# GpSimd issues the stores and loads of the pieces it splits, in the head attentions of a four-layer kernel

## The chip, the cores and the metric

The kernel is one program on one NeuronCore of a Trainium2 chip. The engines are named as in the profile: PE is TensorE, with its weight loads apart as PEld; DVE is VectorE; ACT is ScalarE; POOL is GpSimd; SP is SyncE, which computes nothing and only issues DMAs. An engine with a small q behind its name (SPq) stands for its instruction queue. The metric is the time of one execution in microseconds (us) on the device. Smaller is better.

## The reference, cut to what matters

Four layers act on x of 4 batches x 512 rows x 256. Each is a gated cross-attention to a context of 4 x 1601 rows, followed by a gated feed-forward part:

```
x = x + tanh(g_xattn[l]) * attention_l(layernorm(x), ctx)
x = x + tanh(g_ffn[l])   * ffn_l(layernorm(x))
```

The attentions of layers 0, 1 and 2 have 16 heads of width 16, and they are what the change is about:

```
q = (x @ Wq + bq) heads;  k = (ctx @ Wk + bk) heads;  v = (ctx @ Wv + bv) heads
layer 1:  q, k = rotary(q), rotary(k)
attention = softmax(q k^T * scale) v @ Wo + bo
```

Layer 3 has one wide head. The feed-forward parts are a quantised linear layer and three mixtures of experts. None of these is changed.

## The kernel before, in words

**Work.** A head attention goes through 4 batches b, and in a batch through 4 groups g of 4 heads. For a group, PE computes all scores once for the row maxima (matmuls `m`, L1289), DVE reduces them (`mxp`, L1172), and three rows with the negated maximum are sent by SP into the augmented queries (`qaug<-tm`, L1047, in layer 0 L894). Then PE computes the scores again, 128 keys at a time and transposed, with the maximum already subtracted (`s`, L1311, a unit called `s2`). ACT takes the exponential (`e_t`, L1403) and PE multiplies by the values (`pv`, L1325). There are 13 x 4 such `s2` units in a group. The maxima of a later group run between the `s2` units of the present one.

**Splitting.** Matmuls take bf16, so each f32 value of q and k is split into three bf16 pieces. `head_split` takes a tile of 128 x 512 from `kf` (and `kr`, for rotary), makes the pieces `ks`, and `split3` writes them (L1054 to L1057). There are two sets of these buffers (f = 0 and 1) and they alternate. `store_parts` then writes the pieces to DRAM, six slots for each row, with three DMAs (3, 2 and 1 slots, hence 384, 256 and 128 KB), and a later `fetch` reads them back into `kaug` and `qaug` in the order that the matmuls want. The tile of a batch b + 1 is split while batch b is computed. POOL splits nearly all: in layer 0 eight tiles of keys and two of queries for each further batch, in layers 1 and 2 two tiles of queries for each batch, and eight tiles of keys for batches 2 and 3. The keys of batches 0 and 1 of layers 1 and 2 are split ahead, during the layer before. In layer 0 the tile comes from PE and ACT. In layers 1 and 2 a tile of keys comes from DRAM (`kf<-keys`, in layer 1 also two halves of `kr<-keys`).

**Order.** `Plan` writes one list of units, and every engine goes through this list in order and does its part of each unit. SP's parts are all DMAs that are not ACT's: `turn` (`qaug<-tm`), `fetch`, the load of the next batch's values (at the unit `take` of the last group, `vn<-values`, L973), and `sum`, which moves the softmax denominators (`rc<-z`, L914) and the outputs (`ot<-z`, L917) once ACT has copied the group's result (`z`, L1415). After `sum` follow, at fixed places in the list: on DVE the reciprocal (`rec`, L1195), on ACT two DMAs (`low`: `sums<-rc`, `spread`: `ot<-sums`), and after each second group on DVE the normalisation (`norm`, L1199). DVE needs the landed DMA there, and the maxima stand behind it.

**SP and the splits.** At a `q` or `k` unit SP waits until POOL or DVE has split the tile, and issues the three stores. In layer 0 it does so at the tile's own unit. In layers 1 and 2 (`head_ready_sp`) it stores the tile of the unit before (`held`), and loads the tile of keys for the next unit (`load`). All of SP's later units wait behind. In layer 2 ACT also issues writes of zeros, 2 MB each, from a unit `take` of a batch after the first on (`xregion<-zero`), which go through ACT's queue q10 like `sums<-rc` and `ot<-sums`.

SP's queue is q1, POOL's is q0.

Of the kernel before, what the change touches and what calls it, by code (L numbers as in the profile page):

```python
# [12 lines left out]
B, T, D, S2 = 4, 512, 256, 1601  # L13
# [780 lines left out]
def head_dma_counts(a, name):  # L794

    a.dmas[name] = a.dmas.get(name, 0) + 1
    return a.dmas[name]


def head_stored(a, u):  # L800

    before = a.dmas.get(f"stored{u.f}", 0)
    a.dmas[f"stored{u.f}"] = before + len(RUNS)
    a.stored_of[u.kind, u.b, u.k, u.j] = (u.f, before, before + len(RUNS))


def head_sp(kn, a):
# [7 lines left out]
    split = {n: sig("split_" + n) for n in ("pool", "dve")}  # L815
    row = lambda t: t.rearrange("(c p) n -> p c n", p=P)
    n_of = lambda name: head_dma_counts(a, name)
    a.ctx_of, a.arrived, a.stored_of = {}, {}, {}
    ctx_until = [None] * 4
    if a.ready:  # L820
        head_ready_sp(kn, a, n_of)
# [25 lines left out]
    for at, u in enumerate(plan.units):  # L847
        if u.kind == "begin":
            if u.b:
                for n_c in range(2):  # L850
                    context(u.b, n_c, (n_c + 1) % 2)
            for by, n in set(a.arrived.values()):
                sp.wait_ge(sig(by, DMA).sem, sig(by, DMA).at(n))
        elif u.kind == "chunk":
            if u.b and u.k + 2 < len(CHUNKS):
                context(u.b, u.k + 2, (u.k + 3) % 2)
        elif u.kind in ("q", "k"):
            c0, n = CHUNKS[u.k] if u.kind == "k" else (0, T)
            dst = w["kparts"] if u.kind == "k" else w["qparts"]
            sp.wait_ge(split[u.by].sem, split[u.by].at(u.n + 1))  # L860
            store_parts(sp, u.kind, dst[P * u.j:P * u.j + P, :, c0:c0 + n], a.split_at[u.f][2][:, :, 0:n], stored[u.f].sem)
            head_stored(a, u)
        elif u.kind == "loads":
            mask_sp(kn, a)
            for t, src in ((a.wv, row(w["wv"])), (a.wo, row(w["wo"])), (a.bv, w["bv"]),
                           (a.bob, w["bo"].rearrange("(a n) -> a n", a=1).to_broadcast([P, D]))):
                sp.dma_start(t[:], src).then_inc(ld.sem, DMA)
        elif u.kind == "fetch":
            by = sig(u.by, DMA)
            for f in range(4):  # L870
                if a.dmas.get(f"stored{f}"):
                    sp.wait_ge(stored[f].sem, stored[f].at(a.dmas[f"stored{f}"]))
            if u.b:
                read = plan.find("s2", b=u.b - 1, g=u.g, k=KT - 1, j=HG - 1).s
                sp.wait_ge(s_full.sem, s_full.at(read + 1))
            h0, h1 = HG * HD * u.g, HG * HD * (u.g + u.k)
            for it, to, src in (("q", a.qaug, "qparts"), ("k", a.kaug, "kparts")):
                if it in u.what:
                    sp.dma_start(to[0:R_MASK, u.g:u.g + u.k, :, :].rearrange("p g j k -> p (g j) k"),
                                 w[src][h0:h1, :, :].rearrange("(h d) s k -> (d s) h k", d=HD)).then_inc(by.sem, DMA)  # L880
                    n_of(u.by)
            if a.mask is not None and "k" in u.what:
                for j in range(HG * u.k):
                    sp.dma_start(a.kaug[R_MASK:R_MASK + 1, u.g + j // HG, j % HG, :],
                                 a.mask[0][u.b:u.b + 1, :]).then_inc(by.sem, DMA)
                    n_of(u.by)
            for n in range(u.k):
                a.arrived[u.b, u.g + n, "k" if "k" in u.what else "q"] = (u.by, a.dmas[u.by])
        elif u.kind == "sum":
            head_sum_sp(kn, a, u)  # L890
        elif u.kind == "turn":
            sp.wait_ge(m_free.sem, m_free.at(u.m + 1))
            for k in range(3):
                sp.dma_start(a.qaug[R_MAX + k:R_MAX + k + 1, u.g, :, :].rearrange("a j (c q) -> a (j c) q", q=P),  # L894
                             a.tm[16 * k:16 * k + 16, :]).then_inc(td.sem, DMA)
# [24 lines left out]
def head_ready_sp(kn, a, n_of):  # L920
# [9 lines left out]
    row = lambda t: t.rearrange("(c p) n -> p c n", p=P)  # L930

    piece = lambda t: t.rearrange("(c t h i) s k -> c t h i s k", c=DC, t=2, h=H // DC)
    splits = [x for x in plan.units if x.kind in ("q", "k")]
    held = []

    def store():

        if held:
            x = held.pop()
            (c0, n), to = (CHUNKS[x.k], keys) if x.kind == "k" else ((0, T), queries)  # L940
            sp.wait_ge(split[x.by].sem, split[x.by].at(x.n + 1))
            store_parts(sp, x.kind, to[x.b, P * x.j:P * x.j + P, :, c0:c0 + n], a.split_at[x.f][2][:, :, 0:n], stored[x.f].sem)
            head_stored(a, x)

    def load(x):

        arrived, (c0, n) = sig(f"kl{x.f}", DMA), CHUNKS[x.k]
        kf, kr, _ = a.split_at[x.f]
        if rope and "tables_k" not in a.dmas:
            left_values()  # L950
            sp.dma_start(a.turn_k[:], a.rope[1]).then_inc(tables_k.sem, DMA)
            n_of("tables_k")
        src = kn.dram["keys"][x.b, P * x.j:P * x.j + P, c0:c0 + n]
        if x.b in LEFT:
            for f in range(a.p.RING):
                kept = sig(f"p_k{f}", DMA)
                sp.wait_ge(kept.sem, kept.at(a.p.stores[f]))
        sp.dma_start(kf[:, 0:n], src).then_inc(arrived.sem, DMA)
        for r in (0, P // 2) if rope else ():
            sp.dma_start(kr[r:r + P // 2, 0:n], src[P // 2 - r:P - r, :]).then_inc(arrived.sem, DMA)  # L960
        for _ in range(a.key_loads):
            n_of(f"kl{x.f}")

    def left_values():

# [13 lines left out]
    for u in plan.units:  # L979
# [19 lines left out]
            sp.wait_ge(filled.sem, filled.at(2))  # L999
            values_of(0)  # L1000
        elif u.kind in ("q", "k"):
            store()
            held.append(u)
            after = splits[splits.index(u) + 1:][0:1]
            for x in after:
                if x.kind == "k":
                    load(x)
        elif u.kind == "fetch":
            by = sig(u.by, DMA)
            if "q" in u.what:  # L1010
                store()
                for f in range(2):
                    last = max(n for (_, b, *_), (at, _, n) in a.stored_of.items() if b == u.b and at == f)
                    sp.wait_ge(stored[f].sem, stored[f].at(last))
            if u.b:
                read = plan.find("s2", b=u.b - 1, g=u.g, k=KT - 1, j=HG - 1).s
                sp.wait_ge(s_full.sem, s_full.at(read + 1))
# [42 lines left out]
def head_split(kn, a, u, eng, name):  # L1060

    own = name + "_own"
    s_free, done = kn.sema("s_free"), kn.sema("split_" + name)
    stored = kn.sema(f"stored{u.f}", DMA)
    n = CHUNKS[u.k][1] if u.kind == "k" else T
    kf, kr, ks = a.split_at[u.f]
    src, o = kf[:, 0:n], kr[:, 0:n]
# [14 lines left out]
        kn.settle(eng, own, eng.tensor_tensor(src, src, o, ALU.add))  # L1082
    if live:
        kn.settle(eng, own, eng.tensor_tensor(src, src, a.mask[1][:, u.b:u.b + 1].to_broadcast([P, n]), ALU.mult))
    before = a.stored_of[u.kind, u.b, u.k, u.j][1]
    if before:
        eng.wait_ge(stored.sem, stored.at(before))
    split3(kn, eng, own, kn.cst["ones"][:, 0:1].to_broadcast([P, n]), o, src, [ks[:, k, 0:n] for k in range(3)],
           a.rope is None and not live and not (a.ready and u.kind == "k")).then_inc(done.sem, 1)

# [1 line left out]
def head_pool(kn, a):  # L1092
    pool, plan = kn.nc.gpsimd, a.plan
    filled, b_made, biased = kn.sema("filled"), kn.sema("b_made"), kn.sema("biased")
    i = pool.memset(a.fill[0:R_ALL - R_MASK, 0:S2], 1.0)
    if not a.ready:
        i = pool.memset(a.fill[0:1, S2:2 * S2], 0.0)
# [11 lines left out]
    for u in plan.units:  # L1109
        if u.kind == "stats":  # L1110
            norm_pool(kn, "n", *FIRST_TILES[u.k], u.k)
        elif u.kind in ("q", "k") and u.by == "pool":
            head_split(kn, a, u, pool, "pool")
        elif u.kind == "bias":

            pool.wait_ge(b_made.sem, b_made.at(3))
            for b in range(B):
                xb = kn.x[:, TT * b:TT * b + TT, :]
                pool.tensor_tensor(xb, xb, a.bob[:].rearrange("p (t n) -> p t n", t=1).to_broadcast([P, TT, D]),
                                   ALU.add).then_inc(biased.sem, 1)  # L1120
# [216 lines left out]
def head_act(kn, a):  # L1337
# [10 lines left out]
    for u in plan.units:  # L1348
# [8 lines left out]
        elif u.kind == "q" or u.kind == "k" and not a.ready:  # L1357
# [8 lines left out]
            for t, (to, b_) in enumerate(zip((kf, kr), bias)):  # L1366
                slot = a.s_slot[(u.s + t) % 3]
                act.wait_ge(s_full.sem, s_full.at(u.s + t + 1))
                i = act.activation(to[:, 0:n], slot[:, 0:n], ACT.Identity, bias=b_[:, u.j:u.j + 1], scale=mul)
                if direct:  # L1370
                    before = a.stored_of[u.kind, u.b, u.k, u.j][1]
                    if before:
                        stored = kn.sema(f"stored{u.f}", DMA)
                        act.wait_ge(stored.sem, stored.at(before))
                    i = act.activation(ks[:, 0, 0:n], slot[:, 0:n], ACT.Identity, bias=b_[:, u.j:u.j + 1], scale=mul)  # L1375
                i.then_inc(s_free.sem, 1)
        elif u.kind == "prep":
# [1724 lines left out]
```

## Time and profile before

| | us |
|---|---|
| median of 3 runs | 3853.88 |
| the runs | 3853.88, 3861.94, 3851.54 |
| span of the profiled execution | 3829.6 |
| median less the span | 24.3 |
| PE busy, share of the span | 3401.9, 89% |
| DVE busy | 2159.4, 56% |
| ACT busy | 2034.7, 53% |
| POOL busy | 745.3, 19% |

The span runs from the first to the last instruction in the profile. What lies around it (start and end of the execution) isn't in the trace; the profiled execution gives no other time of its own, so the difference to the median of the runs stands for it. The attention of layer 0 lies between about 100 and 860 us, that of layer 1 between 1030 and 1805 us, and that of layer 2 between 2110 and 2880 us.

### The profile page before, as it was taken

Reading aid. Unit: us, or ns where it says so; the run is one execution under the profiler, and the core shown is the slowest. Engines: PE = TensorE matmul, PEld = TensorE weight load, DVE = VectorE, ACT = ScalarE, POOL = GpSimd, SP = SyncE. Lnnn points to the kernel's source line nnn. Section 1 sums busy time; section 2 is a strip of 40 time slices with the busy share of each in tenths; the row PEclk is TensorE's granted clock in tenths of the full one; section 3 lists DMA queues with packets and bytes.
Section 4 is the critical chain, followed back from the end, with each engine's and each line's share of the span. In section 5 each row is a group of like instructions: output and inputs, shape, how many; then the busy total and the mean of one; then the engine's idle time right before and its main releaser. Section 6 shows DMA issues by size and latency. Waiting matters only on the chain.

```text
span 3829.6 us, 52360 instructions
## 1 busy us (share of the span) xinstructions
PE 3401.9 (89%) x18396; PEld 1770.7 (46%) x18396; DVE 2159.4 (56%) x3463; ACT 2034.7 (53%) x4490; POOL 745.3 (19%) x768
## 2 busy tenths in 40 slices
PE   5899999988689989997899799989987979987997
PEld 3333333325432323332697322323326956687996
DVE  6767676736757777873402477767743033264333
ACT  2566666763236666775333266667772322244664
POOL 2211111003635331000302141210002010022332
PEclk8999999999779999998899799999998989999998
DMA  8132424105664443211874655644208521042554
GB/s 194 42 103 61 106 57 110 26 14 187 178 182 124 101 111 82 45 24 46 267 231 154 185 152 118 171 112 103 77 10 285 186 78 69 1 143 92 184 186 167
DMA packets 314686, 456.02 MB, mean 119 GB/s; under 512 B 66315, under 2 KB 234195, under 8 KB 312251
## 3 DMA queue, kind: packets, MB, share of 16 engines
q1 hardware_dynamic: 233206, 285.70, 27.5%
q0 software_dynamic: 29568, 104.65, 8.2%
q10 hardware_dynamic: 51653, 62.32, 5.8%
q8 instruction: 150, 2.46, 0.3%
q14 instruction: 109, 0.89, 0.1%
HBM read 292.46 MB, written 153.91 MB: 117 GB/s over the span
## 4 chain that ended last, share of the span: by engine, by line
PE 67%; DVE 13%; DMA 8%; ACT 4%; POOL 3%; issue 3%; SPq 1%; ACTq 0%; another core or an unknown queue 0%; POOLq 0%; DVEq 0%
PE pv L1325 14%; PE m L1289 11%; PE s L1311 9%; DVE mxp L1172 9%; PE h L2811 5%; PE y L2819 5%; PE h L2385 4%; PE y L2394 4%; PE y L1791 2%; PE s L1771 2%; PE s L1256 2%; DMA sums<-rc 2%; ACT e_t L1403 1%; DMA ot<-sums 1%; PE m L1333 1%
## 5 line engine op out<-in xcount | busy, mean ns | idle before, releaser
L1172 DVE TENSOR_REDUCE mxp<-m 128x1 f32<-128x802 f32 x1536 | 1447.8, 987 | 526.9 <-PE m L1289 523.2
L1403 ACT ACTIVATE e_t<-s 128x512 f32<-128x512 f32 (+1 forms) x2496 | 1340.3, 599 | 552.0 <-PE s L1311 532.9
L1289 PE MATMUL m<-kaug,qaug 97*128 97x401 bf16 x3072 | 811.6, 347 | 97.5 <-DVE mxp L1172 51.6
L1311 PE MATMUL s<-qaug,kaug 100*128 100x512 bf16 (+1 forms) x2496 | 859.4, 386 | 34.1 <-ACT e_t L1403 29.0
L1325 PE MATMUL pv<-e_t,v 128*32 128x512 f32 (+1 forms) x4992 | 670.3, 609 | 0.2
L1311 PEld LDWEIGHTS s<-qaug,kaug 100*128 100x128 bf16 (+1 forms) x2496 | 229.4, 99 | 733.8 <-ACT e_t L1403 519.6
L1289 PEld LDWEIGHTS m<-kaug,qaug 97*128 97x128 bf16 x3072 | 273.4, 99 | 506.7 <-DVE mxp L1172 265.2
L127 POOL TENSOR_TENSOR rstd<-rstd,mhalf 128x16 f32<-128x16 f32 (+2 forms) x9 | 24.2, 2690 | 1150.8 <-DVE rstd L120 1150.8
L2881 ACT ACTIVATE ez<-h,b 128x128 f32<-128x128 f32 x440 | 120.1, 388 | 159.7 <-PE h L2811 159.7
L1325 PEld LDWEIGHTS pv<-e_t,v 128*32 128x32 f32 (+1 forms) x4992 | 98.6, 108 | 214.9 <-ACT e_t L1403 161.3
L2272 DVE SCALAR_TENSOR_TENSOR y<-y,b 128x256 f32<-128x256 f32 x39 | 16.6, 425 | 303.0 <-PE y L2394 303.0
L2683 DVE TENSOR_SCALAR ez<-ez 128x1024 f32<-128x1024 f32 x55 | 38.2, 694 | 224.6 <-ACT z L2881 224.6
L1055 POOL TENSOR_TENSOR kr<-kf,ks 128x512 f32<-128x512 f32 (+1 forms) x78 | 78.4, 1005 | 432.2 <-ACT ks L1375 428.1
L2468 ACT ACTIVATE hT<-h,b 128x128 f32<-128x128 f32 x312 | 84.9, 383 | 128.1 <-PE h L2385 128.0
L2385 PE MATMUL h<-xtT,w 128*128 128x128 f32 x1248 | 149.3, 279 | 0.3 <-ACT xtT L2485 0.3
L2819 PE MATMUL y<-w,hT 128*128 x624 | 143.0, 383 | 5.8 <-DVE hT L2684 5.8
L2811 PE MATMUL h<-xtT,w 128*128 128x128 f32 x1248 | 147.3, 277 | 0.0
L2385 PEld LDWEIGHTS h<-xtT,w 128*128 128x128 f32 x1248 | 146.3, 196 | 0.6 <-ACT xtT L2485 0.5
L2811 PEld LDWEIGHTS h<-xtT,w 128*128 128x128 f32 x1248 | 144.1, 194 | 0.1
L2394 PE MATMUL y<-w,hT 128*128 x624 | 140.9, 379 | 0.0
L2819 PEld LDWEIGHTS y<-w,hT 128*128 128x128 f32 x624 | 116.8, 192 | 20.9 <-issue 6.4
L2881 ACT ACTIVATE z<-h,b 128x128 f32<-128x128 f32 x440 | 122.8, 453 | 0.0
(377 smaller groups left out, 3616.2 us busy)
## 6 DMA issues: line engine op xcount, KB each, us to landing
w<-in_L_w POOLq DMA_DIRECT2D x78, 1024.0 KB, 5.4
w<-in_L_w SPq DMA_DIRECT2D x24, 1024.0 KB, 12.7
xregion<-zero ACTq DMA_DIRECT2D x10, 2056.0 KB, 12.2
kaug<-kparts SPq DMA_DIRECT2D x16, 1200.8 KB
kaug<-kready SPq DMA_DIRECT2D x32, 600.4 KB
kaug<-kready SPq DMA_DIRECT2D x16, 1200.8 KB
vn<-values SPq DMA_DIRECT2D x8, 1536.0 KB
values<-p_vb ACTq DMA_DIRECT2D x21, 512.0 KB
```

Of the source, the lines that this page charges most:

```text
L1055: kn.settle(eng, own, eng.tensor_tensor(rest, src, parts[0], ALU.subtract))
L1172: dve.tensor_reduce(a.mxp[:, u.g % 2, half, n:n + 1], a.m_slot[u.m % 2][:].rearrange("p (a n) -> p a n", a=2)[:, :, 0:PIECE + 1], AX.XY, A ...
L1289: m = pe.matmul(slot[:, 512 * k:512 * k + PIECE + 1], a.qaug[0:R_MAX, u.g, j, P * qc:P * qc + P], a.kaug[0:R_MAX, u.g, j, k0:k0 + PIECE + ...
L1311: pe.matmul(slot[0:KW[u.k], :], a.kaug[0:R_ALL, u.g, u.j, P * u.k:P * u.k + KW[u.k]], a.qaug[0:R_ALL, u.g, u.j, :], start=True, stop=True) ...
L1325: m = pe.matmul(a.pv[32 * j:32 * j + 32, :], a.v[0:KW[u.k], u.k, u.g, VW * j:VW * j + 32], a.e_t[0:KW[u.k], u.n % 2, j, :], start=u.k == 0 ...
L1403: act.activation(a.e_t[0:KW[u.k], e % 2, u.j, :], a.s_slot[u.s % 3][0:KW[u.k], :], ACT.Exp).then_inc(s_free.sem, 1)
L2385: m = pe.matmul(a.h_slot[i % 2][:, P * f:P * f + P], a.w1[:, w1_at, c, P * f:P * f + P], xT(c), start=c == 0, stop=c == DC - 1)
L2394: m = pe.matmul(a.y_slot[i % 2][:, 0:D], a.hT[:, i % 2, f, :], w2(f), start=f == 0, stop=f == FC - 1)
L2468: t = act.activation(a.hT[:, p, f, :], slot[:, P * f:P * f + P], func, bias=bias(f))
L2811: m = pe.matmul(a.h_slot[i % 2][:, P * f:P * f + P], w1[:, c, P * f:P * f + P], xT(c), start=c == 0, stop=c == DC - 1)
L2819: m = pe.matmul(a.y_slot[i % 2][:, 0:D], a.hT[:, i % 2, f, :], w2(f), start=f == 0, stop=f == FC - 1)
L2881: t = act.activation(to[:, p, P * f:P * f + P], slot[:, P * f:P * f + P], func, bias=bias(f))
```

## The change

SP no longer stores the tiles that POOL splits, and no longer loads keys. POOL does both itself, right behind the split. `head_stores_itself` is true for every tile that POOL splits, other than those of batch 0 in layer 0. After a split and its stores, in layers 1 and 2, POOL issues the load of the tile after the next, which goes into the buffers that it has just read. SP's `fetch` waits for the new semaphores `pooled0` and `pooled1` beside the old ones. In layers 1 and 2 SP now stores the one tile that DVE splits at its own unit. Loads and stores are the same in number, size and place; three stores a tile, one load (three in layer 1) a tile of keys, and once the rotary table `turn_k`, go from q1 to q0.

```diff
+def head_stores_itself(a, u):
+    return u.by == "pool" and (a.ready or u.b > 0)
+
+def head_store_pool(kn, a, u):
+    pool, done, stored = kn.nc.gpsimd, kn.sema("split_pool"), kn.sema(f"pooled{u.f}", DMA)
...
+    pool.wait_ge(done.sem, done.at(u.n + 1))
+    store_parts(pool, u.kind, dst, a.split_at[u.f][2][:, :, 0:n], stored.sem)
+
+def head_load_pool(kn, a, x):
...
+    if rope and "tables_k" not in a.dmas:
...
+        pool.dma_start(a.turn_k[:], a.rope[1]).then_inc(kn.sema("tables_k", DMA).sem, DMA)
...
+    pool.dma_start(kf[:, 0:n], src).then_inc(arrived.sem, DMA)
+    for r in (0, P // 2) if rope else ():
+        pool.dma_start(kr[r:r + P // 2, 0:n], src[P // 2 - r:P - r, :]).then_inc(arrived.sem, DMA)
...
 head_sp, layer 0:
-            sp.wait_ge(split[u.by].sem, split[u.by].at(u.n + 1))
-            store_parts(sp, u.kind, dst[...], a.split_at[u.f][2][:, :, 0:n], stored[u.f].sem)
+            if not head_stores_itself(a, u):
+                sp.wait_ge(...); store_parts(sp, ...)
             head_stored(a, u)
...
         elif u.kind == "fetch":
-                if a.dmas.get(f"stored{f}"):
+                for name in (f"stored{f}", f"pooled{f}"):
...
 head_ready_sp, layers 1 and 2:
         elif u.kind in ("q", "k"):
-            store()
-            held.append(u)
-            after = splits[splits.index(u) + 1:][0:1]
-            for x in after:
-                if x.kind == "k":
-                    load(x)
+            store(u)
...
 head_pool:
             head_split(kn, a, u, pool, "pool")
+            if head_stores_itself(a, u):
+                head_store_pool(kn, a, u)
+            for x in splits[splits.index(u) + 2:][0:1] if a.ready else ():
+                if x.kind == "k":
+                    head_load_pool(kn, a, x)
```

## Rows read from the trace of the kernel before

**Rows 1.** The page's first line

```profile
span 3829.6 us, 52360 instructions
```

**Rows 2.** SP's own waits, all of the run: engine line, releaser, us in total, times, longest us

```profile
SPq L94 <- POOL ks L1057: 258.2, 44, 19.5
```

**Rows 3.** Timeline of SP: start us, us, line, operation; the issues of `rc<-z`

```profile
1297.75 0.60 SPq L914 DMA_DIRECT2D rc<-z  x1
...
1354.34 0.59 SPq L914 DMA_DIRECT2D rc<-z  x1
...
1397.29 0.59 SPq L914 DMA_DIRECT2D rc<-z  x1
...
1475.26 0.60 SPq L914 DMA_DIRECT2D rc<-z  x1
...
1566.31 0.61 SPq L914 DMA_DIRECT2D rc<-z  x1
```

**Rows 4.** Timeline of ACT at 1347 us, the copy of `z`

```profile
1347.00 0.59 ACT L1415 COPY z<-pv 128x512 f32<-128x512 f32 x1 [0.76 <-PE pv L1325]
```

**Rows 5.** Timeline of SP, 1340 to 1363 us

```profile
1349.65 2.31 SPq L94 DMA_DIRECT2D kready<-ks  x3
```

**Rows 6.** Timeline of DVE, three of the reciprocals; in brackets idle time before

```profile
176.60 0.25 DVE L1195 RECIPROCAL rc<-rc 128x16 f32<-128x16 f32 x1 [1.38 <-DMA rc<-z]
...
1186.97 0.25 DVE L1195 RECIPROCAL rc<-rc 128x16 f32<-128x16 f32 x1 [2.18 <-DMA rc<-z]
...
1364.06 0.25 DVE L1195 RECIPROCAL rc<-rc 128x16 f32<-128x16 f32 x1 [7.71 <-DMA rc<-z]
```

**Rows 7.** Timeline of POOL, 221 to 240 us

```profile
224.32 0.31 POOL L1057 TENSOR_TENSOR ks<-kr,ks 128x65 bf16<-128x65 f32 x1
...
229.88 1.16 POOL L1055 TENSOR_TENSOR kr<-kf,ks 128x512 f32<-128x512 f32 x1 [5.25 <-ACT ks L1375]
...
235.84 1.16 POOL L1057 TENSOR_TENSOR ks<-kr,ks 128x512 bf16<-128x512 f32 x1
```

**Rows 8.** Timeline of SP, 222 to 243 us

```profile
233.42 5.48 SPq L94 DMA_DIRECT2D qparts<-ks  x6
...
241.19 0.47 SPq L879 DMA_DIRECT2D kaug<-kparts  x1
```

**Rows 9.** Waits of PE up to 3000 us: us in total, times, longest us

```profile
PE m L1289 <- DMA kaug<-kparts: 22.4, 4, 11.4
```

**Rows 10.** Groups of POOL by line: busy us, mean ns, idle before

```profile
L2618 POOL DMA_DIRECT2D w<-in_L_w x39 | 28.2, 722 | 13.5 <-PE h L2811 11.7 <-issue 1.5
...
L2626 POOL DMA_DIRECT2D xt<-xregion x39 | 22.1, 566 | 26.9 <-issue 26.9
```

**Rows 11.** Timeline of POOL, 3504 to 3513 us

```profile
3507.81 0.55 POOL L2626 DMA_DIRECT2D xt<-xregion  x1 [0.42 <-issue]
```

**Rows 12.** DMA issues of the whole run: count, KB each, median us to landing

```profile
yback<-y,dest POOLq DMA_INDIRECT x39, 2.4
...
qparts<-ks SPq DMA_DIRECT2D x8, 128.0 KB, 2.7
```

**Rows 13.** Timeline of SP, the two loads of the next batch's values, layer 1

```profile
1329.29 0.58 SPq L973 DMA_DIRECT2D vn<-values  x1
...
1493.81 0.60 SPq L973 DMA_DIRECT2D vn<-values  x1
```

**Rows 14.** Waits, 1494:1510, 2380:2402 and 2555:2580 us

```profile
DVE ot L1199 <- DMA ot<-sums: 2.5, 1, 2.5
...
DVE ot L1199 <- DMA ot<-sums: 7.6, 1, 7.6
...
DVE ot L1199 <- DMA ot<-sums: 10.6, 1, 10.6
```

**Rows 15.** DMA queues from 2383 to 2392 us: packets, MB, share of 16 engines

```profile
q10 hardware_dynamic: 1649, 1.70, 90.5%
...
q1 hardware_dynamic: 319, 0.44, 20.0%
```

More of the change, by code:

```diff
@@ L800, in head_stored @@
 def head_stored(a, u):
-    before = a.dmas.get(f"stored{u.f}", 0)
-    a.dmas[f"stored{u.f}"] = before + len(RUNS)
-    a.stored_of[u.kind, u.b, u.k, u.j] = (u.f, before, before + len(RUNS))
+    name = f"pooled{u.f}" if head_stores_itself(a, u) else f"stored{u.f}"
+    n = a.dmas.get(name, 0) + len(RUNS)
+    a.dmas[name] = n
+    a.stored_of[u.kind, u.b, u.k, u.j] = (name, n, a.stored_last.get(u.f))
+    a.stored_last[u.f] = (name, n)
+def head_stores_itself(a, u):
+    return u.by == "pool" and (a.ready or u.b > 0)
+def head_store_pool(kn, a, u):
+    pool, done, stored = kn.nc.gpsimd, kn.sema("split_pool"), kn.sema(f"pooled{u.f}", DMA)
+    (c0, n), to = (CHUNKS[u.k], "k") if u.kind == "k" else ((0, T), "q")
+    if a.ready:
+        dst = kn.dram["kready" if to == "k" else "qready"][u.b, P * u.j:P * u.j + P, :, c0:c0 + n]
+    else:
+        dst = a.w[to + "parts"][P * u.j:P * u.j + P, :, c0:c0 + n]
+    pool.wait_ge(done.sem, done.at(u.n + 1))
+    store_parts(pool, u.kind, dst, a.split_at[u.f][2][:, :, 0:n], stored.sem)
+def head_load_pool(kn, a, x):
+    pool, arrived, (c0, n), rope = kn.nc.gpsimd, kn.sema(f"kl{x.f}", DMA), CHUNKS[x.k], a.rope is not None
+    kf, kr, _ = a.split_at[x.f]
+    if rope and "tables_k" not in a.dmas:
+        for f in range(2):
+            kept = kn.sema(f"p_v{f}", DMA)
+            pool.wait_ge(kept.sem, kept.at(len(a.p.chunks) // 2))
+        pool.dma_start(a.turn_k[:], a.rope[1]).then_inc(kn.sema("tables_k", DMA).sem, DMA)
+        head_dma_counts(a, "tables_k")
+    src = kn.dram["keys"][x.b, P * x.j:P * x.j + P, c0:c0 + n]
+    if x.b in LEFT:
+        for f in range(a.p.RING):
+            kept = kn.sema(f"p_k{f}", DMA)
+            pool.wait_ge(kept.sem, kept.at(a.p.stores[f]))
+    pool.dma_start(kf[:, 0:n], src).then_inc(arrived.sem, DMA)
+    for r in (0, P // 2) if rope else ():
+        pool.dma_start(kr[r:r + P // 2, 0:n], src[P // 2 - r:P - r, :]).then_inc(arrived.sem, DMA)
+    for _ in range(a.key_loads):
+        head_dma_counts(a, f"kl{x.f}")
 def head_sp(kn, a):
@@ L859, in head_sp @@
             dst = w["kparts"] if u.kind == "k" else w["qparts"]
-            sp.wait_ge(split[u.by].sem, split[u.by].at(u.n + 1))
-            store_parts(sp, u.kind, dst[P * u.j:P * u.j + P, :, c0:c0 + n], a.split_at[u.f][2][:, :, 0:n], stored[u.f].sem)
+            if not head_stores_itself(a, u):
+                sp.wait_ge(split[u.by].sem, split[u.by].at(u.n + 1))
+                store_parts(sp, u.kind, dst[P * u.j:P * u.j + P, :, c0:c0 + n], a.split_at[u.f][2][:, :, 0:n], stored[u.f].sem)
             head_stored(a, u)
@@ L870, in head_sp @@
             for f in range(4):
-                if a.dmas.get(f"stored{f}"):
-                    sp.wait_ge(stored[f].sem, stored[f].at(a.dmas[f"stored{f}"]))
+                for name in (f"stored{f}", f"pooled{f}"):
+                    if a.dmas.get(name):
+                        sp.wait_ge(sig(name, DMA).sem, sig(name, DMA).at(a.dmas[name]))
             if u.b:
@@ L932, in head_ready_sp, with store @@
     piece = lambda t: t.rearrange("(c t h i) s k -> c t h i s k", c=DC, t=2, h=H // DC)
[L933 to L939, printed above, removed]
+    def store(x):
+        if not head_stores_itself(a, x):
             (c0, n), to = (CHUNKS[x.k], keys) if x.kind == "k" else ((0, T), queries)
@@ L942, in store @@
             store_parts(sp, x.kind, to[x.b, P * x.j:P * x.j + P, :, c0:c0 + n], a.split_at[x.f][2][:, :, 0:n], stored[x.f].sem)
[L943 to L962, printed above, removed]
+        head_stored(a, x)
     def left_values():
@@ L1010, in head_ready_sp @@
             if "q" in u.what:
-                store()
                 for f in range(2):
-                    last = max(n for (_, b, *_), (at, _, n) in a.stored_of.items() if b == u.b and at == f)
-                    sp.wait_ge(stored[f].sem, stored[f].at(last))
+                    for name in (f"stored{f}", f"pooled{f}"):
+                        of_b = [n for (_, b, *_), (at, n, _) in a.stored_of.items() if b == u.b and at == name]
+                        if of_b:
+                            sp.wait_ge(sig(name, DMA).sem, sig(name, DMA).at(max(of_b)))
             if u.b:
@@ L1063, in head_split @@
     s_free, done = kn.sema("s_free"), kn.sema("split_" + name)
-    stored = kn.sema(f"stored{u.f}", DMA)
     n = CHUNKS[u.k][1] if u.kind == "k" else T
@@ L1084, in head_split @@
         kn.settle(eng, own, eng.tensor_tensor(src, src, a.mask[1][:, u.b:u.b + 1].to_broadcast([P, n]), ALU.mult))
-    before = a.stored_of[u.kind, u.b, u.k, u.j][1]
+    before = a.stored_of[u.kind, u.b, u.k, u.j][2]
     if before:
-        eng.wait_ge(stored.sem, stored.at(before))
+        stored = kn.sema(before[0], DMA)
+        eng.wait_ge(stored.sem, stored.at(before[1]))
     split3(kn, eng, own, kn.cst["ones"][:, 0:1].to_broadcast([P, n]), o, src, [ks[:, k, 0:n] for k in range(3)],
@@ L1094, in head_pool @@
     filled, b_made, biased = kn.sema("filled"), kn.sema("b_made"), kn.sema("biased")
+    splits = [x for x in plan.units if x.kind in ("q", "k")]
     i = pool.memset(a.fill[0:R_ALL - R_MASK, 0:S2], 1.0)
@@ L1370, in head_act @@
                 if direct:
-                    before = a.stored_of[u.kind, u.b, u.k, u.j][1]
+                    before = a.stored_of[u.kind, u.b, u.k, u.j][2]
                     if before:
-                        stored = kn.sema(f"stored{u.f}", DMA)
-                        act.wait_ge(stored.sem, stored.at(before))
+                        stored = kn.sema(before[0], DMA)
+                        act.wait_ge(stored.sem, stored.at(before[1]))
                     i = act.activation(ks[:, 0, 0:n], slot[:, 0:n], ACT.Identity, bias=b_[:, u.j:u.j + 1], scale=mul)
```

2 lines of the change are left out of this document (1 added, 1 removed).

## The prediction

> **What bounds the kernel now.** The page comes first: the span is 3829.6 us [rows 1], PE is busy for 89% of it and POOL for 19%, so more work on POOL is not in itself a cost. Then the waits by engine. SP's own list shows that it stood 258.2 us in 44 waits for a split of POOL [rows 2]. That is not a cost yet: SP is a queue, and what counts is which of its later DMAs somebody needed. So I went through the issues of `rc<-z` in the timeline of SP. ACT had `z` ready at 1347.59 [rows 4], and SP issued the move only at 1354.34 [rows 3], because at 1349.65 it was still storing pieces that POOL had just finished [rows 5], with a fetch behind them. DVE then stood 7.71 us before its reciprocal [rows 6], the maxima behind it stood too, and PE and ACT ran dry. Two smaller waits of the kind are at 1187 us (2.18 us) and 176.6 us (1.38 us) [rows 6]. The other 40-odd sums aren't late by SP.
>
> The second thing to see is a chain in layer 0 that has no slack. POOL splits the two query tiles of the next batch directly after each other: the first from 229.88, the second ends at 235.84 + 1.16 = 237.00 [rows 7]. SP issues six stores in 5.48 us from 233.42 on, thus to 238.90, and 2.3 us later, at 241.19, it can issue the fetch [rows 8]. PE waits for this fetch: the list of PE's waits has 22.4 us in four for `kaug<-kparts`, of which the longest, 11.4 us, is the start of the kernel. The other three, 11.0 us together or 3.7 each, are the fetches for batches 1 to 3 [rows 9]. Whatever delays that fetch is added to the end.
>
> **Cost 1, the chain of layer 0.** POOL must now issue three DMAs between the first query tile and the second. The trace of before has no such store from POOL. The nearest rows are its loads: 566 ns for 128 rows (`xt`) and 722 ns for 256 rows (`w`) [rows 10]. By these I put the three stores, with 384, 256 and 128 runs of 1 KB, at 0.88 + 0.72 + 0.57 = 2.2 us. Between two DMAs POOL shows 0.42 us idle [rows 11], so three cost 3.4 us. From below, three at 0.57 without a gap are 1.7 us. From above, three like the largest with gaps are 3.9 us. I take 3.4, as the gap is in the row.
> This hits at three points. (a) Before the queries come two short tiles of keys; the second ended at 224.32 + 0.31 = 224.63 [rows 7]. With two stores of 3.4 us before the queries POOL is free at 231.4 and not before 229.88, so 1.5 us late (0 to 2.6). (b) The second query tile starts 3.4 us later (1.7 to 3.9). (c) Its own stores take POOL until 3.4 us after the split, where SP was done after 238.90 - 237.00 = 1.9 us: 1.5 us more (0 to 2.0). I take the landing as unchanged: POOL's indirect DMA of 128 KB lands 2.4 us after its start, SP's store of 128 KB after 2.7 [rows 12]. Sum 6.4 us for a batch (1.7 to 8.5), three batches: **+19.2 us** (5 to 25.5). Nothing covers it, since PE waits already.
>
> The Trainium skill, "DMA: Bandwidth & Descriptors", sections "Issuing engine by pattern" and "Specifications", sends simple loads and stores to SyncE and gives about 1 us to the first byte from GpSimd and 0.6 from SyncE; by that the landing would be 0.4 us later, an estimate of 1.2 us more for three batches. Rows 12 show no such difference, and I don't count it.
>
> **Gain 1, sums in layer 0.** SP no longer stands before `sum` of group 0. The wait of 1.38 us [rows 6] goes, in three batches: **-4.2 us** (0 to -5).
>
> **Gain 2 and its give-back, layer 1.** Without the wait SP issues the fetch as soon as the previous group's scores are done, and `rc<-z` at 1347.6. It had 8.7 us to land (DVE was ready at 1364.06 - 7.71 = 1356.35). The wait of 7.71 goes. But SP also reaches the load of the next batch's values earlier. In batch 0 to 1 it stood behind the splits until 1329.29, in batch 1 to 2, where no keys are split between, it went out at 1493.81 [rows 13], next to the DMA for the normalisation, and DVE stood 2.5 us for that [rows 14]. After the change both boundaries look alike, so the second is the measure of the first. From the sum of the last group to the second sum after it: 1397.29 - 1297.75 = 99.5 us in the first, 1566.31 - 1475.26 = 91.1 in the second [rows 3]. The difference holds the gain and what is given back: **-8.5 us** (8.5 + 2.5 = -11 if the values don't collide, -2 if the sum is late anyway). By the same account a DVE wait of 7.71 us cost 11, 1.4 times itself, so for the 2.18 us at 1187 [rows 6] I take 1.4 x 2.18: **-3 us** (0 to -4).
>
> **Cost 2, layer 2.** No sum is late here. But the values go out earlier in batch 0 to 1 as well. DVE waits 7.6 us there for the normalisation's DMA and 10.6 at the next boundary, where the values already go out beside it [rows 14]. The difference is 3.0; half of it I take as real, since PE and ACT have a little work queued: **+1.5 us** (0 to 3).
>
> **Cost 3, POOL's transfers among the others.** SP paced the loads of keys; now POOL runs eight tiles back to back, and stores its query tiles at once. At the two boundaries of layer 2 this falls into the clearing writes. **+2 us** (0 to 9, which is 1 MB or so more in front of each of two landings and of ACT's waits for `sums<-rc`).
>
> Free edits: POOL's other DMAs (some 260 outside the layer 0 chain) cost some 1.1 us each, and lie in POOL's idle four fifths of the span; where that cover is gone it shows as in cost 1. The first tile's store at the start of layers 1 and 2 is some 1.5 us later under the preparing matmuls. SP's two more waits in `fetch` cost nothing by themselves.
>
> **Sum.** 19.2 - 4.2 - 8.5 - 3 + 1.5 + 2 = +7.0 us on 3829.6 gives 3836.6 in the span. The median of the runs shown is 24.3 us above the span of this execution, and I add the same: **3861 us**.
>
> **Rivals.**
> *The stores of POOL are nearly free (faster).* One mechanism, at the second query tile of layer 0: if descriptors are made while POOL computes, cost 1 falls to its lower bound of 5 us, and the gains remain: 5 - 4.2 - 8.5 - 3 = -10.7, and with the full 11 for gain 2, -13.2: 3841 us. It decides as soon as a query tile starts less than 2 us after the last one's end. For it: POOL's DMA rows last only 0.6 to 0.7 us. Against it: the gap of 0.42 between them. 0.18.
> *Transfers in turn (slower).* Until now SP's ring was held up behind ACT's: while q10 had 90.5% of the DMA engines from 2383 to 2392 us, q1 had 20% [rows 15]. If POOL's ring takes a part beside both, the landings that DVE and ACT wait for in layers 1 and 2 go late, cost 3 is its upper 9: 3868, and up to 3876 if layer 1's sums are pushed out as well. It decides when `ot<-sums` lands over 2 us later than now. 0.20. The Trainium skill, "DMA: Bandwidth & Descriptors", section "Queues, rings and completion order", says that each DMA engine goes round the queues with work, a packet of each. By that rule POOL's transfers slow SP's and ACT's evenly. The trace agrees only in part, as rows 15 are far from even.
> *It doesn't do what it says in layer 1.* The fetch stands before `rc<-z` in the same queue still, and with POOL's stores beside it the sum lands after 1356.35. Gain 2 shrinks to 2 and the small one to 0: +7 + 6.5 + 3 = 3870 us. Against it: the sums from 1397 us on wait for nothing with the same fetch ahead. 0.12.
>
> **Numbers.** My forecast has 0.50, with its own range 3852 to 3870. About 0.3% (11.6 us) is what a measurement of this kernel tells from no change: 3842 to 3865. The forecast lies inside with 0.37 and above with 0.13; the free stores are faster with 0.15 and the same with 0.03; the transfers in turn slower with 0.18 and the same with 0.02; the late sum slower with 0.09 and the same with 0.03. Faster 0.15, same 0.45, slower 0.40. The range of 8 in 10 reaches from 3845, inside the first rival, to 3877.
>
> **What would show it.** Cost 1: a gap of some 3.4 us on POOL between the two query tiles at 230 to 240 us, the fetch at about 247 and not 241, and the three waits of PE for `kaug<-kparts` some 6 us longer each. Gain 2: no wait of DVE before the reciprocal at about 1360, 91 us and not 99.5 over these two groups. Cost 2: `vn<-values` at the first boundary right after ACT's copy, and a wait for `ot<-sums` of 2 us in layer 1 and about 10 in layer 2. It would be wrong if POOL's DMA costs far from 1.1 us, if the store lands much later than SP's, or if POOL's burst of key tiles makes other waits than those named.

## The result, and the profile after

The changed kernel takes 3888.45 us (median of 4 runs, 3883.22 to 3893.53) against 3855.32 (4 runs) for the kernel before: ratio 1.0077 with a 95% interval of 1.0057 to 1.0098, thus 22 to 38 us slower. The forecast was 3861 us, with 3845 to 3877 as its range. The sign of its sum (+7) was right. Its size was not, and the time lies above the range.

The page's first rows of the kernel after, the pages' rows of two queues (packets, MB, share of 16 engines; first before, then after) and SP's waits after:

```profile
span 3882.0 us, 52370 instructions
...
PE 3419.7 (88%) x18396; PEld 1777.1 (46%) x18396; DVE 2162.8 (56%) x3463; ACT 2033.7 (52%) x4490; POOL 941.3 (24%) x1061
```

```profile
q1 hardware_dynamic: 233206, 285.70, 27.5%
q0 software_dynamic: 29568, 104.65, 8.2%
```

```profile
q1 hardware_dynamic: 163878, 224.05, 21.9%
q0 software_dynamic: 49520, 166.30, 13.1%
```

```profile
SPq L94 <- POOL ks L1073: 17.5, 1, 17.5
```

The change does what it says. SP's waits for splits of POOL went from 44 to 1 [rows 2]. POOL has 196 us more of work (745.3 before), and about 62 MB moved from SP's queue (q1) to POOL's (q0). In q1 these bytes were 69328 packets, in q0 they are 19952: the same data goes in some 3.5 times fewer and larger packets. That matters below.

**Two spans that can't be subtracted.** The spans of the two traces differ by 52.4 us [rows 1], the medians by 33. The profiled run after took 3883.22 us with its span of 3882.0, so only 1.2 us lie outside a span. So the 24.3 us that the prediction added as "what lies around" didn't lie around it: with 1.2 us around its span of 3829.6 the profiled execution of before lies 21 us under the fastest timed run of before, 3851.54. It was a fast one, by luck or because it ran on another chip; the record doesn't say which. The control below shows where it was faster.

**Layer 0.** PE's waits for the fetch, and POOL's timeline at the same place as [rows 7]:

```profile
PE m L1311 <- DMA kaug<-kparts: 33.2, 4, 13.2
```

```profile
229.27 2.08 POOL L94 DMA_DIRECT2D kparts<-ks  x3 [0.29 <-POOL ks L1073]
232.15 1.15 POOL L1071 TENSOR_TENSOR kr<-kf,ks 128x512 f32<-128x512 f32 x1 [0.80 <-ACT ks L1397]
...
235.95 2.10 POOL L94 DMA_DIRECT2D qparts<-ks  x3 [0.30 <-POOL ks L1073]
238.06 1.17 POOL L1071 TENSOR_TENSOR kr<-kf,ks 128x512 f32<-128x512 f32 x1
...
240.42 1.15 POOL L1073 TENSOR_TENSOR ks<-kr,ks 128x512 bf16<-128x512 f32 x1
241.88 2.08 POOL L94 DMA_DIRECT2D qparts<-ks  x3 [0.30 <-POOL ks L1073]
```

and SP's issue of the fetch, which answers to [rows 8]:

```profile
246.76 0.47 SPq L922 DMA_DIRECT2D kaug<-kparts  x1
```

The waits grew from 22.4 us [rows 9] to 33.2. The longest of the four is the start of the kernel, which the change doesn't touch (11.4, then 13.2 us); the other three, the fetches of the chain, grew from 11.0 to 20.0 us. Three stores take POOL 2.1 us back to back, with one gap of 0.3 before the first and none between them. The stores of the key tiles cost nothing: at 232.15 POOL had already waited 0.80 us for ACT.

**Layer 1.** Issues of `rc<-z` and `vn<-values` in SP's timeline, then DVE's timeline:

```profile
1303.68 0.62 SPq L957 DMA_DIRECT2D rc<-z  x1
1321.13 0.34 SPq L993 DMA_DIRECT2D vn<-values  x1
...
1360.56 0.61 SPq L957 DMA_DIRECT2D rc<-z  x1
1401.33 0.62 SPq L957 DMA_DIRECT2D rc<-z  x1
```

```profile
1332.85 0.69 DVE L1221 TENSOR_TENSOR ot<-ot 128x512 f32<-128x512 f32 x1 [4.61 <-DMA ot<-sums]
1371.46 0.25 DVE L1217 RECIPROCAL rc<-rc 128x16 f32<-128x16 f32 x1 [2.15 <-DMA rc<-z]
```

`rc<-z` goes out as soon as `z` is there, and DVE's wait for it fell from 7.71 us [rows 6] to 2.15. But the values now go out at 1321, beside the normalisation's DMA, and DVE stands 4.61 us for that, where the kernel before shows no such wait. The two groups take 1401.33 - 1303.68 = 97.7 us. They took 99.5 [rows 3]. By ACT's copies of `z`, the group over the boundary grew from 49.9 to 56.9 us and the next one fell from 49.7 to 40.8: the gain came, and most of it was given back.

**Layer 2.** Most of the cost is here, as the experiments show. ACT's timeline over one group boundary, POOL's stores there, and the DMA queues in four windows of it (2270 to 2276, 2278 to 2286, and of the latter 2278 to 2279 and 2280 to 2281 us; the times of packets overlap, so shares can add up to over 100%):

```profile
2268.71 0.66 ACTq L1463 DMA_DIRECT2D xregion<-zero  x1
...
2272.20 0.33 ACTq L1445 DMA_DIRECT2D sums<-rc  x1
...
2288.07 0.57 ACTq L1452 DMA_DIRECT2D ot<-sums  x1
2288.69 2.56 ACT L1425 ACTIVATE e_t<-s 128x512 f32<-128x512 f32 x5 [9.78 <-DMA sums<-rc]
```

```profile
2269.48 2.09 POOL L94 DMA_DIRECT2D kready<-ks  x3 [0.30 <-POOL ks L1073]
...
2277.07 0.81 POOL L94 DMA_DIRECT2D kready<-ks  x1 [0.30 <-POOL ks L1073]
```

```profile
q10 hardware_dynamic: 1421, 1.46, 108.8%
```

```profile
q0 software_dynamic: 456, 1.39, 75.6%
q10 hardware_dynamic: 602, 0.47, 30.0%
```

```profile
q0 software_dynamic: 41, 0.16, 79.3%
q10 hardware_dynamic: 44, 0.05, 28.7%
```

```profile
q0 software_dynamic: 63, 0.19, 77.1%
q10 hardware_dynamic: 61, 0.06, 28.4%
```

ACT writes 2 MB of zeros (`xregion<-zero`) and, behind it in the same queue (q10), the 8 KB of sums. A few instructions on, `ot<-sums` waits until these have landed, and the exponentials stand behind it. From 2270 to 2276 us only ACT's queue moves, 1.46 MB, though POOL issued 768 KB of pieces at 2269.48. Then both move, and the counts of packets are even (41 to 44, 63 to 61), but POOL's packets are three to four times as large: ACT's queue, at 0.19 MB a us just before (2275 to 2276 us), is down to 0.05. `ot<-sums` goes out 15.9 us after the issue of the sums (2288.07 - 2272.20), and ACT stands 9.78 us.

What that does to PE is seen in PE's timeline and in the windows (us, PE busy and count, granted clock, DMA share, GB/s):

```profile
2289.34 1.10 PE L1333 MATMUL s<-qaug,kaug 100*128 100x512 bf16 x2 [8.47 <-ACT e_t L1425]
```

```profile
2268.00:2280.00 12.00, 11.81 (x71) 1.00 0.95 207
...
2288.00:2292.00 4.00, 2.66 (x12) 0.50 0.22 58
2292.00:2296.00 4.00, 3.74 (x24) 0.86 0.11 27
```

PE had a granted clock of 1.00 (2.4 GHz) while it was busy, stood 8.47 us, and came back at 0.50 (1.2 GHz). So this stall cost its own length and a slow stretch after it. The same happens at the first group boundary of the next batch (ACT stands 7.74 us before 2480.28); at the other boundaries between groups of this layer ACT stands 2.95 to 3.32 us for the sums.

### The profile page after: what moved, and what is told of

Read it like the earlier page. It is cut to its first block, busy times and chain, and to the rows that moved or that the text cites. A ratio compares the mean times of both kernels' runs of the same rounds, so it can differ in the third digit from the quotient of the medians.

```text
span 3882.0 us, 52370 instructions
## 1 busy us (share of the span) xinstructions
PE 3419.7 (88%) x18396; PEld 1777.1 (46%) x18396; DVE 2162.8 (56%) x3463; ACT 2033.7 (52%) x4490; POOL 941.3 (24%) x1061
## 3 DMA queue, kind: packets, MB, share of 16 engines
q0 software_dynamic: 49520, 166.30, 13.1%
## 4 chain that ended last, share of the span: by engine, by line
PE 67%; DVE 14%; DMA 9%; ACT 4%; issue 3%; POOL 2%; SPq 1%; ACTq 0%; POOLq 0%; DVEq 0%
PE pv L1347 14%; PE m L1311 11%; PE s L1333 9%; DVE mxp L1194 9%; PE h L2833 5%; PE y L2841 5%; PE h L2407 4%; PE y L2416 3%; PE y L1813 2%; PE s L1793 2%; DMA sums<-rc 2%; PE s L1278 2%; DMA ot<-sums 2%; ACT e_t L1425 1%; PE m L1355 1%
## 5 line engine op out<-in xcount | busy, mean ns | idle before, releaser
L127 POOL TENSOR_TENSOR rstd<-rstd,mhalf 128x16 f32<-128x16 f32 (+2 forms) x9 | 24.3, 2696 | 1150.2 <-DVE rstd L120 1150.2
## 6 DMA issues: line engine op xcount, KB each, us to landing
xregion<-zero ACTq DMA_DIRECT2D x10, 2056.0 KB, 12.7
```

## The experiments

All variants are written into the changed kernel with a switch for each layer; the ratios are to the kernel before, run on the same chip. Its median there was 3867 to 3872 us, and not 3855, so experiments are compared by these ratios. The kernel after itself wasn't run on these chips.

```diff
 def head_stores_itself(a, u):
-    return u.by == "pool" and (a.ready or u.b > 0)
+    return u.by == "pool" and (a.ready or u.b > 0) and u.kind in POOL_STORES[a.layer]
...
-            for x in splits[splits.index(u) + 2:][0:1] if a.ready else ():
+            for x in splits[splits.index(u) + 2:][0:1] if a.ready and POOL_LOADS[a.layer] else ():
```

Where a switch is off, SP has its old `store` and `load` back, in the old order.

**1. Control.** `POOL_STORES = {0: '', 1: '', 2: ''}`, `POOL_LOADS` off.

> All stores and loads back on SyncE in the three attentions, written into the kernel after the change with the same edits that the partial variants use. Both theories: within 0.3% of the kernel before (ratio 0.997 to 1.003). Its profile is a second execution of the old order of work: if its span is near 3850 and not near 3830, some 20 of the 52 us by which the two traces differ are a matter of the execution; if a control is over 0.3% from before, the other variants are to be read against it and not against before.

Measured: 3869.46 us, ratio 1.0003 (0.9994 to 1.0012). The switches cost nothing that shows. The span of its profile is 3863.3 us, with the same order of work as the 3829.6 of before. The first group boundary of layer 2 in both, first the kernel before, then the control (ACT's timeline):

```profile
2266.95 2.56 ACT L1403 ACTIVATE e_t<-s 128x512 f32<-128x512 f32 x5 [3.08 <-DMA sums<-rc]
```

```profile
2249.80 0.58 ACT L1485 COPY z<-pv 128x512 f32<-128x512 f32 x1 [0.76 <-PE pv L1395]
...
2274.02 2.56 ACT L1473 ACTIVATE e_t<-s 128x512 f32<-128x512 f32 x5 [3.96 <-DMA sums<-rc]
...
2292.77 0.58 ACT L1485 COPY z<-pv 128x512 f32<-128x512 f32 x1 [0.76 <-PE pv L1395]
```

ACT stood 0.9 us longer in the control. PE stood 1.78 us there in the kernel before and 2.66 in the control (PE's timeline), and the windows just after it read:

```profile
2268.00:2272.00 4.00, 3.66 (x22) 1.00 0.08 31
```

```profile
2274.00:2278.00 4.00, 3.23 (x15) 0.81 0.10 35
```

The first is the kernel before, which kept its clock; the second is the control, which did not. Its group took 43.0 us from one `z` to the next, and that of before 40.9. From its first to its last `z` the attention of layer 2 is 23 us longer in the control's trace (647 against 624), some two thirds of the 34 us between the spans. The length of the stall alone doesn't decide, though. In the nine traces with the clears early (before, after, experiments 1 to 6 and 9) ACT stands 70 times for `sums<-rc` in this layer, and PE behind it, each time from a clock of 1.00. After 16 of these stalls of PE (1.05 to 2.48 us) the clock stayed at 1.00, after the other 54 (1.65 us and more) it fell within the next 8 us: between 1.65 and 2.48 us both happened. The groups took 40.2 to 41.6 us where it stayed and 42.1 us or more where it fell. In the profile of before it stayed in all six, in the control it fell in all eight. The clears landed a little earlier in the former, too (12.2 us against 13.1 in the median). So the trace of before hid how little room was left in this layer.

**2. Layer 0 alone.** `POOL_STORES = {0: 'qk', 1: '', 2: ''}`

> Only the attention of layer 0 has GpSimd's own stores. Theory A (the cost lies in the transfers of layer 2): about +11 us, the growth of the offset in layer 0 by the trace, ratio 1.003. Theory B (the prediction: the cost is the chain of layer 0, three fetches each 6.4 us late, less 4.2): +15 us, ratio 1.004. Both: PE's three waits for kaug<-kparts together 8 to 20 us longer; layer 2 keeps the group times of before.

Measured: 3875.35 us, ratio 1.0021 (1.0012 to 1.0029), +8 us (4.6 to 11). PE's waits for the fetch, which were 23.2 us in the control:

```profile
PE m L1359 <- DMA kaug<-kparts: 34.0, 4, 14.0
```

Without the start of the kernel (13.8 us in the control, 14.0 here) three fetches grew from 9.4 to 20.0 us, 3.5 for each. The chain of layer 0 is real, and a little over half the size that was forecast.

**3. Layer 1 alone.** `{0: '', 1: 'qk', 2: ''}`, with the loads of layer 1

> Only the attention of layer 1 has GpSimd's stores and loads. Theory A: 0 to -4 us, since the trace shows -3.4 over this attention, ratio 0.999 to 1.000. Theory B: -11.5 us, ratio 0.997, as the late sum is gone and the give-back is small.

Measured: 3865.29 us, ratio 0.9994 (0.9982 to 1.0007), -2 us (-7 to +3). The attention of this layer is 6 us shorter in its trace than in the control's. A gain of 11.5 us is excluded.

**4. Layer 2 alone.** `{0: '', 1: '', 2: 'qk'}`, with the loads of layer 2

> Only the attention of layer 2 has GpSimd's stores and loads. Theory A (a third ring takes its turns at the DMA engines beside ScalarE's clearing writes of 2 MB, and the small moves queued behind these land late): +20 to +34 us, ratio 1.005 to 1.009, with ACT's waits for sums<-rc of 5 us and more in several groups. Theory B: +3 us, ratio 1.001, and the rest of the 34 us that the trace shows in this layer is a matter of the execution.

Measured: 3890.91 us, ratio 1.0061 (1.0048 to 1.0074), +24 us (19 to 29). Experiments 2 to 4 add up to 30 us (to 26 if each is counted from the control), of the 33 (22 to 38) of the whole change. In the trace the layer is 16 us longer from its first to its last `z` than in the control: the first groups of batches 0 and 1 by 6.8 and 7.7 us, the groups over the two batch boundaries, where the forecast saw the cost, by 2.2 and 3.2, and the others 4 us shorter together. The first boundary again (ACT's timeline; 49.8 us between the two `z`):

```profile
2260.67 0.59 ACT L1485 COPY z<-pv 128x512 f32<-128x512 f32 x1 [0.76 <-PE pv L1395]
...
2291.39 2.55 ACT L1473 ACTIVATE e_t<-s 128x512 f32<-128x512 f32 x5 [10.46 <-DMA sums<-rc]
...
2310.48 0.59 ACT L1485 COPY z<-pv 128x512 f32<-128x512 f32 x1 [0.76 <-PE pv L1395]
```

and POOL's store of the tile that falls behind the clear:

```profile
2271.54 2.12 POOL L94 DMA_DIRECT2D kready<-ks  x3 [0.30 <-POOL ks L1120]
```

**5 and 6. Layer 2, stores alone and loads alone.** `{2: 'qk'}` with the loads off, and `{2: ''}` with the loads on, each behind the split that frees its buffer.

> Layer 2 alone, and only the stores of the split pieces are GpSimd's; SyncE loads the keys, each after the previous split, as before. Theory A1 (the extra ring's bytes and runs beside ScalarE's clears cost; the stores are about four fifths of the DMAs and of the small runs): +15 to +20 us of the 24 that layer 2 alone cost. Theory A2 (the pace: GpSimd loads its next keys at once and so runs its eight tiles in a burst, where SyncE spaced them): 0 to +5 us.

> Layer 2 alone, and only the loads of the keys are GpSimd's; SyncE stores the pieces after its waits, as before. Theory A1: +3 to +8 us, the smaller part. Theory A2: +15 to +20 us, if the pace of the loads is what matters.

Measured: stores 3878.25 us, ratio 1.003 (1.0019 to 1.0041), +12; loads 3869.76, ratio 1.0004 (0.9993 to 1.0015), +2. The two don't add up to 24: some 10 us are missing, a little more than the scatter of the three together. Neither account was right alone: the stores are the larger part, but SP's loads pace them. With SP's loads, which stand in its queue behind other work, the first boundary takes 44.2 us in place of 49.8, and ACT stands 4.80 us for the sums and not 10.46. In experiment 4 POOL stores tiles 0.8 and 8.4 us after the issue of the clear, in experiment 5 5.6 and 12.7 us after it. So the burst, one tile straight after the other with stores and loads, seems to be what puts two whole tiles beside the clear; that is read from one boundary.

**7 and 8. The clears behind the small moves.** In ACT's queue the write of zeros goes behind `ot<-sums`, with the stores by POOL in layer 2 (7) and with everything by SP (8):

```diff
-            if a.clears and u.b:
-                clear_act(kn, a, (u.b - 1) * NG + u.g)
...
         elif u.kind == "spread":
             head_spread_act(kn, a, u)
+            if a.clears:
+                clear_act(kn, a, u.n)
```

> Layer 2 alone, stores and loads by GpSimd, but ScalarE issues its clearing write of a group after the move of the sums and not ahead of it, so that sums<-rc and ot<-sums have no 2 MB in front of them in their own queue. Theory A (the three rings meet, but what makes it dear is the clear ahead of the small moves): at most +5 us over the kernel with late clears alone, against +24 with early clears. Rival (the third ring slows everything alike): still +15 to +25 over the kernel with late clears alone.

> The old order of work (SyncE stores and loads everything) with ScalarE's clears late. It is the base for the run before it. Theory A: faster than before by 10 to 25 us, as DVE's waits of 7.6 and 10.6 us for ot<-sums in layer 2 go with what they drag along. Rival (those waits come from values and keys in SyncE's queue, not from the clears): within 3 us of before.

Measured: (8) 3823.22 us, ratio 0.988 (0.9865 to 0.9896), 46 us faster than before (40 to 52), more than either account expected. In the traces the layer is 47 us shorter than in the control from its first to its last `z` (599.9 against 647.2); half of it lies in the two groups over the batch boundaries (60.0 to 45.9 and 56.7 to 47.2 us), where `ot<-sums` was behind a clear. (7) 3840.84 us, ratio 0.9933 (0.992 to 0.9945): 17.6 us slower than (8). So the clear ahead of the sums is dear in itself, but taking it away doesn't take away the cost of POOL's transfers. That part of my account fell. PE's timeline at the first boundary of (7) and the windows behind it:

```profile
2295.34 0.61 PE L1381 MATMUL s<-qaug,kaug 100*128 100x512 bf16 x1 [3.45 <-DMA qaug<-tm]
```

```profile
2283.00:2291.00 8.00, 7.91 (x50) 2.74 (x50) 6.15 (x9) 5.69 (x11) 0.32 (x1) 1.00 1.00 122
2295.00:2299.00 4.00, 3.67 (x10) 1.34 (x10) 1.99 (x2) 2.02 (x4) 0.00 (x0) 0.50 1.04 220
2299.00:2303.00 4.00, 4.00 (x15) 0.97 (x15) 1.64 (x2) 1.59 (x4) 0.00 (x0) 0.50 0.43 102
```

Columns: us, busy of PE, PEld, DVE, ACT and POOL, granted clock, DMA share, GB/s. Now it is SP's move of the maxima, `qaug<-tm`, that lands late: 9.8 us after its issue in the median, with the clear and POOL's last pieces outstanding, and 6.1 us after it in (8). PE stands 3.45 us, and then its clock is 0.50 for two windows. In (8) the same wait is 0.16 us.

**9 and 10. POOL holds its stores at the sums.** Before it stores a tile, POOL waits until the last group's sums have landed, with the clears early (9) and late (10):

```diff
     pool.wait_ge(done.sem, done.at(u.n + 1))
+    if a.layer == 2:
+        sums = [x for x in a.plan.units[:a.plan.units.index(u)] if x.kind == "spread"]
+        if sums:
+            summed = kn.sema("summed", DMA)
+            pool.wait_ge(summed.sem, summed.at(3 * sums[-1].n + 2))
     store_parts(...)
```

> Layer 2 alone, stores and loads by GpSimd, but the store of a tile whose place in the order of the units is behind a group's sums waits until these sums have landed; so no piece is written between ScalarE's clear and sums<-rc in the groups where keys are split. Theory A (dear are the stores that fall between a clear and the landing of sums<-rc): of the +24 us of layer 2 alone at most +8 are left, and the group from the first to the second z of the layer takes about 43 us, as in the control, and not 49.8. Theory U (GpSimd's transfers cost what they cost wherever they fall): still +18 to +28, the lateness only appears at another landing.

> The same with ScalarE's clears behind the move of the sums. Both the third ring and the clear are then behind the small moves. The base is the kernel with late clears alone (about 44 us below before), against which GpSimd's unguarded transfers cost 18. Theory A: 0 to +8 us over that base, about 35 to 44 below before. Theory U: again +14 to +22 over the base, because the pieces now land late behind the clear and the fetch waits for them.

Measured: (9) 3877.69 us, ratio 1.0016 (1.0006 to 1.0026): +6 us (2 to 10) where the unguarded kernel had +24. POOL stood for the sums, and at this boundary ACT stood no longer than in the control (POOL's, then ACT's timeline):

```profile
2282.00 2.12 POOL L94 DMA_DIRECT2D kready<-ks  x3 [15.45 <-DMA sums<-rc]
```

```profile
2282.10 2.56 ACT L1478 ACTIVATE e_t<-s 128x512 f32<-128x512 f32 x5 [3.70 <-DMA sums<-rc]
```

The boundary took 43.3 us. The same bytes by the same queue, sent 13 us later (23.9 us after the `z`, and not 10.9), cost a quarter. So it was their place, between a clear and the landing of the sums, that made some 18 of the 24 us. (10) 3838.08 us, ratio 0.9919 (0.9906 to 0.9933): 15 us over (8), and 5 us under (7) with intervals that overlap. So with late clears the guard does little: at the first boundary PE again stands for `qaug<-tm`, 4.39 us. Theory U names the fetch there, and that isn't what the trace shows.

**11 and 12. The parts put together.** Clears late, layer 1 by POOL, layer 2 by SP; layer 0 with the key tiles by POOL (11, `{0: 'k', 1: 'qk', 2: ''}`) or all by SP (12).

> A version put together from the parts: layer 0 with the stores of the key tiles alone by GpSimd (the query tiles, which the fetch waits for, by SyncE), layer 1 by GpSimd, layer 2 by SyncE, ScalarE's clears late. If the parts add up: late clears -44, layer 1 -2 to -6, key tiles of layer 0 -2 to 0: 44 to 52 us below before, ratio 0.987 to 0.989. If GpSimd's transfers cost in layer 1 as they do in layer 2: above -44.

> Layer 1 by GpSimd, layers 0 and 2 by SyncE, clears late. Against the run before it this leaves out the key tiles of layer 0. By the account of the prediction (a wait of 1.4 us before the reciprocal, three times) it is 4 us slower than that run; by the account of the trace of layer 0 alone (2 us of gain in all) 2 us slower, too little to tell. Below before by 44 to 50 us.

Measured: (11) 3817.49 us, ratio 0.9867 (0.9852 to 0.9882), 51 us faster than before. (12) 3818.36 us, ratio 0.9865 (0.985 to 0.988). Both beat both kernels. They can't be told from each other, so no gain or loss from the key tiles of layer 0 shows. Against (8) they are 5 us better, with intervals that overlap. Nearly the whole gain is the place of the clears.

## Why the prediction was wrong

- **Cost 3, the step that failed.** "+2 us (0 to 9)" for POOL's transfers among the others. Layer 2 alone measured +24 (19 to 29), against the +3.5 of costs 2 and 3 together. The mechanism is the rival "Transfers in turn", which had 0.20 and at most 9 us; the measured time is above even its 3876. I priced it as a megabyte or so in front of two landings. Three things were missing: most of it falls on ACT's wait for `sums<-rc` at the first group boundary of two batches, where keys are split, and not at the two batch boundaries; what stands in line there is already 2 MB of zeros, with ACT waiting 3 us; and a stall of PE of 8 to 9 us is followed by a stretch at half clock.
- **Rows 15 were read as protection.** ACT's queue had 90.5% beside SP's 20.0% there, and I took it that ACT's queue holds its own. The trace after shows both in the same clear: POOL's queue moves nothing for 6 us with 768 KB issued, and then has 75.6% against 30.0. The rule of the Trainium skill, "DMA: Bandwidth & Descriptors", section "Queues, rings and completion order", that an engine takes a packet of each queue in turn, was nearer to the effect than my reading of one window. From 2278 to 2281 us the trace bears it out, with 41 packets to 44, 58 to 59 and 63 to 61; even in packets is not even in bytes, and there the two queues differ by more than three to one. From 2270 to 2276 us, with 1421 packets to none, it doesn't. The trace of before has the same: SP issued a store at 2383.84, and its queue had no packets from 2385 to 2390 us.
- **Cost 1, layer 0: right chain, half the size.** Forecast +19.2 us, measured 9.0 in PE's three waits (10.6 in layer 0 alone over the control). (a) the key tiles' stores: 1.5 forecast, 0 shown, as POOL waited for ACT after them. (b) between the query tiles: 3.4 forecast. From the start of the first query tile to the end of the second it is 241.57 - 232.15 = 9.42 us and was 7.12 [rows 7], thus 2.3. (c) from there to the issue of the fetch 5.19 us and before 4.19 [rows 7, 8]: 1.0, forecast 1.5. The gap of 0.42 us of rows 11 was the wrong row: three stores have one gap of 0.3. The landing, taken as unchanged, is hardly later: for 384, 256 and 128 KB of `qparts` 3.1, 3.2 and 2.8 us in the median from POOL (kernel after) against 2.6, 2.9 and 2.7 from SP (control).
- **Gain 1.** Forecast -4.2 us. Layer 0 alone costs 8.2 where the waits cost 10.6, so about -2.4. That the waits of 1.38 us went is shown, but their price can't be separated from the scatter.
- **Gain 2, layer 1.** Forecast -11.5 us, measured -2 (-7 to +3). SP's wait before `rc<-z` went, as forecast. The give-back was read off the second boundary, with a wait of DVE of 2.5 us; the wait is 4.61 at the first one, whose group grew by 7.0 us, and 3.5 at the second, whose group grew by 1.8 (trace after). And 2.15 us of DVE's wait for `rc<-z` stayed, which was the third rival in part. The small gain of 3 us came: the group at 1187 us went from 43.7 to 39.7.
- **Cost 2.** +1.5 us. DVE's waits for `ot<-sums` in layer 2 are 6.2 and 13.0 us, in sum 19.2 against 18.2 [rows 14]. That looks right, but the control, with SP's old order, has 10.0 and 10.8, in sum 20.8: no such cost shows. One by one they are not as forecast either ("about 10" for each).
- **The 24.3 us.** They weren't around the span but inside it. The sum itself, 7 against 33, is 26 us short: 20 of it in layer 2, 10 in layer 1, less 7 in layer 0. That leaves 3, which the runs don't resolve. As the 24.3 only carried the sum from a fast execution to the median, they did no harm to it.

What stays open: why POOL's queue moves nothing for the first 6 us of a clear and then a packet for each of ACT's, and what the remaining 6 us of the guarded kernel are. Its two batch boundaries are 2 to 3 us longer than the control's. Nor is it separated how much of the cost lies in the moment of the stores and how much in POOL's queue, with its larger packets: in the control SP issues no store between a clear and the landing of the sums at the first boundary, and no run lets SP send the same burst there.

## What to carry to other kernels

A queue that stands behind somebody's wait is also a pacer: before taking the wait away, look at what its transfers will run beside, and which landing an in-order engine waits for there. The bytes didn't change here, only when, by which queue and in what packets they went, and a guard that held them behind that landing took back three quarters of the cost. And where a bulk write with no deadline stands ahead of an 8 KB move that an engine waits for, put it behind: that was worth 46 us, more than the change cost.

## What the runs showed of the hardware that was not expected

- Two queues share the DMA engines in no fixed proportion: with stores of POOL's queue outstanding, ACT's queue had 1421 packets to none in 6 us, and a few us later 44 to 41. The same bytes were 69328 packets in SP's queue and 19952 in POOL's, so at even counts POOL's queue moved 0.16 MB to ACT's 0.05.
- A stall of PE from full clock of 1.78 us left it at 1.00, one of 2.66 was followed by a window at 0.81, one of 3.45 and one of 8.47 by windows at 0.50. So 0.9 us more of waiting went with 2 us more for a group, in two executions of the same order of work. Over 70 such stalls, those between 1.65 and 2.48 us went either way.
- A store that POOL issues takes it 0.70 us in the mean (384, 256 and 128 KB: 0.81, 0.73, 0.57), and three mostly go back to back; at 2277 us in the trace after there are 0.22 us between the first and the second.
